# Local attention of the last two layers: value halves shifted by DMA, and the rotation of q and k one step earlier, around the softmax's reciprocal

## The reference, cut to what matters

```python
h = shift_token(x)
q, k, v = jnp.split(h @ wqkv, 3, axis=-1)          # 8 heads of 64
q = l2norm(q) * qs;  k = l2norm(k) * ksc
q, k = rotary_xpos(q, k)                            # q*cos*scale + rotate_half(q)*sin*scale
# windows of 64 queries; keys and values: the window and the one before it
sim = jnp.einsum('bhwid,bhwjd->bhwij', bq, bk)      # masked, bq carries QK_SCALE
attn = jax.nn.softmax(sim, axis=-1)
out = jnp.einsum('bhwij,bhwjd->bhwid', attn, bv)
x = x + out @ wo                                    # then the feed-forward
```

## Time and profile before

| | |
|---|---|
| median of 3 runs | 1512.03 us (1510.12 to 1512.65) |
| profiled execution | 1508.53 us, span 1506.5 us, mean granted TensorE clock 0.957 |
| PE busy | 1333.5 us, 89% of the span |
| DVE busy | 1013.3 us, 67% |
| ACT busy | 792.7 us, 53% |
| POOL busy | 361.6 us, 24% |

### The profile page before, as it was taken

The page is one execution under the profiler, slowest core; times in us unless marked ns, Lnnn a source line. Parts: engine busy times, 40 slices in busy tenths (PEclk is TensorE's granted clock), DMA queues, the critical chain, the costliest instruction groups (busy, mean ns, idle before and its releaser), DMA issues.

```text
span 1506.5 us, 23829 instructions
## 1 busy us (share of the span) xinstructions
PE 1333.5 (89%) x9009; PEld 790.8 (52%) x9009; DVE 1013.3 (67%) x2202; ACT 792.7 (53%) x1681; POOL 361.6 (24%) x288
## 2 busy tenths in 40 slices
PE   6999999999999999999589999987279988799886
PEld 4767677776777673333223333333146654366652
DVE  5767767687766856765577667740967775877755
ACT  4544435444444442434136666675169984499851
POOL 0000000011000003335410000000267771477732
PEclk9999999999999999999569999999589999999998
DMA  5000000000000000002023111100200000000000
GB/s 141 1 1 1 1 1 1 1 1 1 1 1 1 0 1 1 1 0 81 29 77 82 46 37 37 36 3 7 57 1 2 2 2 1 1 2 2 2 1 28
DMA packets 23725, 26.03 MB, mean 17 GB/s; under 512 B 5602, under 2 KB 20140, under 8 KB 22316
## 3 DMA queue, kind: packets, MB, share of 16 engines
q1 hardware_dynamic: 23612, 24.51, 5.5%
HBM read 20.11 MB, written 4.39 MB: 16 GB/s over the span
## 4 chain that ended last, share of the span: by engine, by line
PE 64%; ACT 14%; DVE 13%; issue 4%; POOL 2%; DMA 2%; SPq 0%; POOLq 0%; DVEq 0%; ACTq 0%
PE ps L679 13%; PE ps L699 8%; PE ps L714 7%; ACT probsT L2283 6%; PE ps L1051 4%; PE ps L1010 4%; PE ps L1031 3%; DVE negmax L1437 2%; PE ps L888 2%; PE ps L882 2%; PE ps L1182 2%; PE ps L650 2%; ACT v_st L2253 2%; PE ps L1173 2%; PE ps L872 2%
## 5 line engine op out<-in xcount | busy, mean ns | idle before, releaser
L2208 ACT ACTIVATE probsT<-ps 128x512 f32<-128x512 f32 (+1 forms) x304 | 163.6, 576 | 103.7 <-PE ps L1035 91.6
L1437 DVE TENSOR_REDUCE negmax<-ps 128x1 f32<-128x1024 f32 x128 | 150.7, 1219 | 72.5 <-PE ps L699 72.4
L2030 ACT ACTIVATE probs<-ps,negmax 128x1024 f32<-128x1024 f32 x128 | 142.5, 1114 | 80.5 <-DVE negmax L1437 76.5
L2036 ACT COPY probsT<-ps 128x512 f32<-128x512 f32 x128 | 74.8, 584 | 168.2 <-PE ps L714 168.1
L714 PEld LDWEIGHTS ps<-ident,probs 128*128 128x128 f32 x1024 | 114.5, 141 | 66.2 <-issue 44.0
L714 PE MATMUL ps<-ident,probs 128*128 128x128 f32 x1024 | 138.4, 277 | 6.6 <-DVE probsT L1450 3.4
L2360 POOL TENSOR_SCALAR rstd<-mv 128x4 f32<-128x4 f32 (+1 forms) x23 | 5.3, 233 | 578.5 <-DVE mv L1372 578.4
L1010 PE MATMUL ps<-arena 76*128 76x512 bf16 (+3 forms) x384 | 113.6, 355 | 26.4 <-DVE cmax L1705 20.6
L699 PE MATMUL ps<-k_st,q_st 64*128 64x512 f32 x512 | 128.7, 622 | 5.9 <-ACT probs L2030 5.9
L1705 DVE CUSTOM_DVE_ANT_0 k_st<-ps,rel 128x256 f32<-128x256 f32 (+7 forms) x128 | 96.8, 756 | 44.1 <-PE ps L1010 43.2
L1705 DVE CUSTOM_DVE_ANT_0 q_st<-ps,rel 128x256 f32<-128x256 f32 (+7 forms) x128 | 96.7, 756 | 41.9 <-PE ps L1010 41.0
(11 more groups left out here) (245 smaller groups left out, 2565.1 us busy)
## 6 DMA issues: line engine op xcount, KB each, us to landing
arena<-c_parts SPq DMA_DIRECT2D x32, 192.0 KB
arena<-c_parts SPq DMA_DIRECT2D x16, 128.0 KB
arena<-in_L_ffn_w_dram SPq DMA_DIRECT2D x3, 512.0 KB
c_parts<-probsT SPq DMA_DIRECT2D x2, 768.0 KB, 3.5
arena<-in_c_far_dram SPq DMA_DIRECT2D x16, 96.0 KB
c_parts<-work SPq DMA_DIRECT2D x2, 768.0 KB, 11.3
work<-in_L_ffn_wqkv_dram SPq DMA_DIRECT2D x1, 1536.0 KB
x_sb<-in_L_attn_x_dram SPq DMA_DIRECT2D x2, 512.0 KB, 5.9
```

Of the source, the lines that this page charges most:

```text
L1437: dve.tensor_reduce(negmax[:, u:u + 1], s2, AX_X, ALU.max, negate=True).then_inc(s_a_negmax, 1)
L2030: act.activation(probs[:, u % NPB, :], s2, ACT.Exp, bias=negmax[:, u:u + 1], accum_out=rowsum[:, u:u + 1]).then_inc(s_a_exp, 1)
L2208: act.activation(c_p[:, kt % 2, j0:j0 + heads, q0 - kt * P:q0 - kt * P + n], ps[:, 4 + c % 2, 0:heads * n].rearrange("p (h n) -> p h n", n ...
```

## The change

Three things are changed, in the last two layers alone. ScalarE no longer fills `d_vs`: SyncE does it with two DMAs of 64 rows x 512 for each tile, both from `d_va`, and ScalarE, the value product and the DMAs wait for each other by a new semaphore `s_d_vs`. The rotation on VectorE is moved from the start of step t (tile t+2) to its end (tile t+3), waits for the projection and no longer for the squares, and the reciprocal of tile t stands between its first product and its other two. The square on ScalarE is moved from the end of step t (tile t+3) to the place behind the value copy (tile t+2), and waits for the rotation. With them, PE's wait for the copies of the turned queries and keys stands behind the mask instead of ahead of it, GpSimd's sum of the queries is moved to the end of its step (tile t+3), and the pieces at the start of a layer follow.

```diff
@@ sync
+            for l in range(DEPTH):
+                for t in range(TILES):
+                    n, par = TILES * l + t, t % 2
+                    sp.wait_ge(s_d_v, n + 1)
+                    if exists(t, -2):
+                        sp.wait_ge(s_d_o, n - 1)
+                    if n:
+                        sp.wait_ge(s_d_vs, shifted(n))
+                    sp.dma_start(d_vs[0:WIN, par, :], d_va[0:WIN, par, :]).then_inc(s_d_vs, 16)
+                    if exists(t, -1):
+                        sp.dma_start(d_vs[WIN:P, par, :], d_va[WIN:P, 1 - par, :]).then_inc(s_d_vs, 16)
@@ tensor, step
-                        pe.wait_ge(s_d_qT, n + 1)
-                        pe.wait_ge(s_d_kT, n + 1)
...
+                        pe.wait_ge(s_d_qT, n + 1)
+                        pe.wait_ge(s_d_kT, n + 1)
                         for h in range(H2):
...
                         pe.wait_ge(s_d_pT, n)
+                        pe.wait_ge(s_d_vs, shifted(n))
@@ vector, rotate
-                    dve.wait_ge(s_d_sq, n + 1)
+                    dve.wait_ge(s_d_qkp, n + 1)
...
                     dve.tensor_tensor(mA, qk, heads(rot_c[:, t:t + 1, :, :]), ALU.mult)
+                    if between:
+                        between()
                     for d, e in ((0, 32), (32, 0)):
@@ vector, step
-                    if exists(t, 2):
-                        rotate(l, t + 2)
+                    def inverse():
+                        dve.wait_ge(s_d_e, n + 1)
+                        dve.reciprocal(d_rr[:, par, :], d_sum[:, par, :]).then_inc(s_d_rr, 1)
...
                         add_keys(l, t + 2)
-                        norms(l, t + 2)
                     if exists(t, -2):
...
+                    if exists(t, 2):
+                        norms(l, t + 2)
                     if piece:
                         piece()
-                    if exists(t, 0):
-                        dve.wait_ge(s_d_e, n + 1)
-                        dve.reciprocal(d_rr[:, par, :], d_sum[:, par, :]).then_inc(s_d_rr, 1)
+                    if exists(t, 3):
+                        rotate(l, t + 3, inverse)
+                    elif exists(t, 0):
+                        inverse()
@@ scalar, square and step
-                    act.wait_ge(s_d_qkp, n + 1)
+                    act.wait_ge(s_d_m, n + 1)
...
-                        if exists(t, -1):
-                            act.wait_ge(s_d_v, n)
-                            act.copy(d_vs[WIN:P, par, :], d_va[WIN:P, 1 - par, :])
                         act.wait_ge(s_d_vp, n + 1)
-                        act.copy(d_va[:, par, :], ps[:, 3, :])
-                        act.copy(d_vs[0:WIN, par, :], ps[0:WIN, 3, :]).then_inc(s_d_v, 1)
+                        if n >= 2:
+                            act.wait_ge(s_d_vs, shifted(n))
+                        if exists(t, -2):
+                            act.wait_ge(s_d_o, n - 1)
+                        act.copy(d_va[:, par, :], ps[:, 3, :]).then_inc(s_d_v, 1)
+                    if exists(t, 2):
+                        square(l, t + 2)
...
-                    if exists(t, 3):
-                        square(l, t + 3)
@@ gpsimd
+            def add_queries(l, t):
+                    n, par = TILES * l + t, t % 2
+                    kq = d_kq[par]
+                    pool.wait_ge(s_d_m, n + 1)
+                    if exists(t, -2):
+                        pool.wait_ge(s_d_qkt, n - 1)
+                    pool.tensor_tensor(kq[:, 0:INNER], d_mA[:, par, 0:INNER], d_mB[:, par, 0:INNER], ALU.add)\
+                        .then_inc(s_d_add, 1)
...
                     if exists(t, 2):
                         unit_norm(l, t + 2)
+                    if exists(t, 3):
+                        add_queries(l, t + 3)
```

More of the change, by code:

```diff
@@ L424, in build @@
         s_d_addk = sem("s_d_addk")
+        s_d_vs = sem("s_d_vs")
         s_d_s = sem("s_d_s")
@@ L455, in build, with exists, shifted @@
         block = ctx.enter_context(nc.Block())
+        def exists(t, shift):
+            return 0 <= t + shift < TILES
+        def shifted(n):
+            return 16 * (2 * n - (n + TILES - 1) // TILES)
         @block.sync
@@ L561, in build @@
         NU = 2 * QT
-        def exists(t, shift):
-            return 0 <= t + shift < TILES
         def ring(j):
@@ L1765, in tables, with rotate @@
                                                   sc[:, n:n + 1, e:e + 32].to_broadcast([P, QT, 32]), ALU.mult))
-            def rotate(l, t):
+            def rotate(l, t, between=None):
                     n, par = TILES * l + t, t % 2
@@ L1787, in add_keys @@
                     n, par = TILES * l + t, t % 2
+                    if exists(t, -2):
+                        dve.wait_ge(s_d_qkt, n - 1)
                     dve.wait_ge(s_d_m, n + 1)
@@ L1793, in norms @@
                     n, par = TILES * l + t, t % 2
+                    dve.wait_ge(s_d_sq, n + 1)
                     dve.tensor_reduce(ss[:, par, :], d_sq[:, par, :].rearrange("p (h d) -> p h d", d=HD2),
@@ L1889, in _ @@
             norms(0, 1)
+            rotate(0, 2)
             for l in range(DEPTH):
@@ L1938, in _ @@
                     add_keys(l + 1, 0)
-                    norms(l + 1, 0)
                 gated(l, 10)
                 if not last:
+                    norms(l + 1, 0)
                     next_shift(l, 1)
@@ L1958, in _ @@
                     next_shift(l, 2)
+                    rotate(l + 1, 2)
                     next_shift(l, 3)
@@ L2309, in _ @@
                 if l == 0:
-                    for t in range(3):
+                    for t in range(2):
                         square(l, t)
@@ L2330, in _ @@
                     if l + 1 < DEPTH:
-                        if j == 8:
+                        if j == 9:
                             square(l + 1, 0)
@@ L2335, in _ @@
                     act.activation(tpre[:, 1:2], eps_c[:, 0:1], ACT.Exp)
-                    square(l + 1, 2)
         @block.gpsimd
@@ L2478, in _ @@
             pool.wait_ge(s_d_init, 1)
-            def unit_norm(l, t):
+            def add_queries(l, t):
                     n, par = TILES * l + t, t % 2
@@ L2484, in unit_norm @@
                     pool.wait_ge(s_d_m, n + 1)
+                    if exists(t, -2):
+                        pool.wait_ge(s_d_qkt, n - 1)
                     pool.tensor_tensor(kq[:, 0:INNER], d_mA[:, par, 0:INNER], d_mB[:, par, 0:INNER], ALU.add)\
                         .then_inc(s_d_add, 1)
+            def unit_norm(l, t):
+                    n, par = TILES * l + t, t % 2
                     pool.wait_ge(s_d_cl, n + 1)
@@ L2489, in unit_norm @@
                     pool.wait_ge(s_d_addk, n + 1)
+                    pool.wait_ge(s_d_add, n + 1)
                     pool.wait_ge(s_d_rn, n + 1)
-                    v = kq[:, INNER:2 * INNER].rearrange("p (h d) -> p h d", d=HD2)
+                    v = d_kq[par][:, INNER:2 * INNER].rearrange("p (h d) -> p h d", d=HD2)
                     pool.tensor_tensor(v, v, d_rn[:, par, H2:2 * H2].unsqueeze(2).to_broadcast([P, H2, HD2]), ALU.mult)\
@@ L2496, in step, with begin @@
                     n, par = TILES * l + t, t % 2
-                    if exists(t, 0):
-                        v = d_p[:, par, :, :]
-                        pool.wait_ge(s_d_rr, n + 1)
-                        pool.tensor_tensor(v, v, d_rr[:, par, :].unsqueeze(2).to_broadcast([P, H2, P]), ALU.mult)\
-                            .then_inc(s_d_p, 1)
+                    v = d_p[:, par, :, :]
+                    pool.wait_ge(s_d_rr, n + 1)
+                    pool.tensor_tensor(v, v, d_rr[:, par, :].unsqueeze(2).to_broadcast([P, H2, P]), ALU.mult)\
+                        .then_inc(s_d_p, 1)
                     if exists(t, 2):
                         unit_norm(l, t + 2)
-            unit_norm(0, 0)
-            unit_norm(0, 1)
+                    if exists(t, 3):
+                        add_queries(l, t + 3)
+            def begin(l):
+                add_queries(l, 0)
+                unit_norm(l, 0)
+                add_queries(l, 1)
+                unit_norm(l, 1)
+                add_queries(l, 2)
+            begin(0)
             for l in range(DEPTH):
@@ L2515, in _ @@
                 if l + 1 < DEPTH:
-                    unit_norm(l + 1, 0)
-                    unit_norm(l + 1, 1)
+                    begin(l + 1)
             for c in range(NCH):
```

## The result

The median of four runs is 1492.20 us (1490.93 to 1493.52), against 1512.12 before: 19.9 us less, a ratio of 0.9871 with a 95% interval of 0.9854 to 0.9888. The forecast was 1485, its range 1480 to 1497. The change is 1.3% faster, clear of the scatter, by three quarters of what was forecast.

The account below looks back on a forecast made before the run. No engine is full; a loop of waits through ScalarE and TensorE sets the 9.04 us step. Gains 17.8 (24 steps) + 2.4 + 2.5 + 4.2 = 26.9 us off the median 1512.03 give 1485, range 1480 to 1497.

Parts of the forecast that it names:

- the steady steps: The 24 evenly spaced steps of both layers: each falls from 9.04 to 8.3 us, 17.8 us in all.
- the ends: Start of layer 0, passage into layer 1 and late steps of both layers: 2.4, 2.5 and 4.2 us gained.
- point 4: Steady step: TensorE's own work and the chain through ScalarE's two copies meet at the next scores; new length 8.3 us.
- Square and copies: Steady step: square (0.90 us) hidden in ScalarE's wait; two 64-row copies (0.63, at most 0.58) only make room for it.
- the near row: Profile row of a 256 KB DMA taking 2.3 us, taken for each new 128 KB DMA, which would be hidden.
- The rival in which they arrive late: Value copy waits for DMA landings, decisive above 8.4 us: 1515 to 1530, or about 1575; 5%.
- The late reciprocal: Steady step: reciprocal delayed, so probabilities come late; step 8.5 us and 1490, or 8.8 and 1497; 20%.
- The tails: Steps 14 and 15 of each layer: 2.1 us gained a layer, 4.2 in all.
- Point 11: Steps 14 and 15: mask off the path gives 0.5 us each, ScalarE's two copies 1.1 in step 15; 2.1 a layer.
- points 9 and 10: Start of layer 0 and passage into layer 1: squares and masks leave the path, 2.4 and 2.5 us gained.
- Point 9: Start of layer 0: square (0.90) and tile 1's mask (1.01) off the way, tile 0's mask (0.52) too; 2.4 us.
- The joint: Passage from layer 0 to 1: two rotations no longer wait for squares (1.9 us), plus 0.6 for three smaller items; 2.5 us.

Follow-up runs that it names:

- Mask alone: Kernel before, with only TensorE's wait for the copies of turned queries and keys moved behind the mask: 1498.75 us, ratio 0.9915.
- mask undone: Changed kernel with TensorE's wait for the copies of turned queries and keys moved back ahead of the mask: 1503.95 us, ratio 0.9948.
- DMAs alone: Kernel before, with only the two DMAs filling the shifted values in place of ScalarE's two 64-row copies: 1506.44 us, ratio 0.9970.
- e13: Not a run: a time mark, the start of tile 13's first exponential on ScalarE, in each layer.
- e14: Not a run: a time mark, the start of tile 14's first exponential on ScalarE, in each layer.
- three edits: Changed kernel with reciprocal ahead of the rotation, norm clamp on GpSimd, and the very first square ahead of its rotation: 1483.21 us, ratio 0.9812.
- e15: Not a run: a time mark, the start of tile 15's first exponential on ScalarE, in each layer.
- clamp on GpSimd: Changed kernel with the clamp of the norms on GpSimd, right ahead of the power, instead of on VectorE: 1489.57 us, ratio 0.9858.
- reciprocal last: Changed kernel with the reciprocal behind all three products of the rotation: 1500.18 us, ratio 0.9924.
- first square first: Changed kernel where, for the first tile of layer 0 only, the square waits for the projection and the rotation for the square: 1490.68 us.
- e0: Not a run: a time mark, the start of tile 0's first exponential on ScalarE, in each layer.
- e1: Not a run: a time mark, the start of tile 1's first exponential on ScalarE, in each layer.

## Why the prediction was right, and where it was not

The median lies in the range, and the steady steps carried it: of 17.8 us forecast for 24 steps 16.1 came, of 9.1 us forecast for the ends 0.9, and 1.0 more at a place that had no term. That so weak an account of the ends still ended in the range is owed to the width that the range had for the rivals.

- **The steady step, right.** 8.3 was forecast and 8.30 and 8.28 measured; 22 steps gave 16.5 us, 0.75 each. Both chains of point 4 are in the profile: the mask runs in the wait for ACT's copies, and PE is busy in 99% of the window. Mask alone and mask undone are 0.50 and 0.44 us a step, near its own 0.52.
- **Square and copies, right in kind.** The square is hidden (ACT waits 0.71 behind it). That the two copies "only make the room for the square" missed 0.13 us, as the DMAs alone show.
- **DMAs, right.** They land in 2.4 us, near the 2.3 of the near row and the 2.3 that I estimated from the Trainium skill (DMA: Bandwidth & Descriptors, Anatomy of one DMA), although that section gives its fit for DMAs issued by GpSimd and these are SyncE's. No engine waits for one. The rival in which they arrive late never came near its 8.4 us.
- **The late reciprocal.** It had 20%, and was there in one step of three. The clamp did wait for the query sum; the Trainium skill's rule (SBUF — State Buffer, Who interferes with whom), that an SBUF-to-SBUF operation of one input in a fast mode and a GpSimd operation keep each other off for a whole instruction, agrees with the trace: the clamp took 1.10 and ended with the query sum, the second shift copy took 1.41, 1.40 and 1.21 beside GpSimd's sums and scalings and 0.42 without. It did not hold beside GpSimd's power: the shift copy at 1282.12 took 0.42 inside a power that ran from 1281.87 for 3.01 us. The cost in the steady steps was 0.07 us, not the 0.2 of the forecast's step of 8.5.
- **The tails, wrong.** Point 11 forecast 2.1 us a layer and nothing was gained (+1.0, +0.3), and the 12th step, counted among the steady ones, lost 0.2 and 0.3 instead of gaining 0.7. Together that is 7.4 us of the 8.9 by which the sum, 26.9, missed the block's 18.0. Two things in it failed.

First, it took the feed-forward's pieces over from before unchanged: I had seen for the clamp that GpSimd can hold VectorE up, and not for the shift copies that follow it at the same place, nor for the scaling of the maxima in step 14. e13 to e14 was 9.5 before and 9.0 by point 11. With a long shift copy and a scaling of 0.17 it is 9.78 (three edits, clock 1.00), with both long 10.53 (layer 0 of the change).

Second, points 9 and 10 reckon with PE's half clock and point 11 does not. Windows from e14 to e15: layer 0 before; layers 0 and 1 of the change; layer 0 with the clamp on GpSimd (columns as for the steady step):

```profile
1234.39:1247.24 12.85, 7.41 (x114) 5.57 (x113) 7.83 (x30) 8.81 (x26) 5.89 (x7) 1.00 0.01 2
...
1229.19:1241.99 12.80, 8.53 (x110) 6.38 (x111) 8.00 (x30) 7.48 (x23) 4.42 (x5) 0.87 0.05 12
1421.47:1433.95 12.48, 8.64 (x114) 6.99 (x113) 7.94 (x30) 7.49 (x24) 4.40 (x5) 0.86 0.01 1
...
1226.30:1237.38 11.08, 7.22 (x114) 5.61 (x113) 7.95 (x30) 7.49 (x24) 4.41 (x5) 1.00 0.07 15
```

At a granted clock of 1.00 the order of the change has 11.07 to 11.09 us here, in all four places where that happened (both layers with the clamp on GpSimd, layer 1 with the reciprocal last and with the three edits). That is 1.8 less than the 12.85 before, so the 1.6 of point 11 for step 15 was right, and the half clock hid it. Step 14 of layer 1 lost to it too: clock 0.85 and 11.39 us. The kernel before lost 1.2 us in step 15 of layer 1 (14.02 at 0.88). By my estimate from these rows the clock is 3.4 of the 5.5 us that the two tails missed.

It may in part be the change's. Ahead of the second chunk in step 14 PE waits 1.1 to 1.4 us in the kernel before and with mask or DMAs alone, and came back at full speed in all six places; where the wait was 1.8 to 2.4 us it came back at half in 6 of 17. Why in these and not in the others stays open.

- **The head, half.** Point 9 forecast 2.4 and 1.2 was measured. It counted the square that goes and not the one that comes: tile 0's square was hidden behind VectorE's tables, and now stands between its rotation and the second projection, 1.1 us. Shown by the run with the first square first. The half clock from e0 to e1 cost the change another 1.0 us, and was made up for by more gain there than forecast (e0 to e1 is 7.51 at full clock; it was 10.31 before, at 0.83).
- **The joint, wrong in size.** 2.5 forecast, 1.0 measured. The rotations did come 2.1 us sooner (45.03 us after e15 before, 42.95 after, for that of tile 1), but of these only 1.2 reached the first maxima. VectorE, GpSimd and PE there, rows of three timelines:

```profile
1284.94 1.23 DVE L1799 TENSOR_TENSOR probs<-ps,arena 128x1024 f32<-128x1024 f32 x1 [0.96 <-PE ps L1148]
...
1294.15 1.18 DVE L1773 COPY arena<-xT 64x512 f32<-64x512 f32 x1
1295.35 1.64 DVE L1779 TENSOR_TENSOR arena<-arena 128x512 f32<-128x512 f32 x1
...
1293.86 1.18 POOL L2528 TENSOR_TENSOR k_st<-k_st,d_rn 128x512 f32<-128x512 f32 x1 [0.17 <-POOL d_rn L2523]
1295.00 1.45 POOL L2516 TENSOR_TENSOR q_st<-probs 128x512 f32<-128x512 f32 x1
...
1304.12 1.04 PE L1178 MATMUL ps<-rel,ident_b 128*128 128x512 bf16 x2 [5.36 <-ACT probsT L2315]
```

The copy (0.42 alone) and the table product (0.68 alone) each ran into a GpSimd instruction and lost 1.7 us between them; before the change one such collision was there already and cost 0.85 (L1764 at 1301.48 took 1.60, elsewhere 0.75), so 0.9 more was lost than before: the part of the 2.1 that is missing. And PE, idle for 5.36 us, did the mask of tile 1 at half speed, as the forecast had allowed for, but stayed there through the scores too: the granted clock from e0 to e1 of layer 1 is 0.64, 0.88 before.

- **The last stretch.** The 1.0 us after e15 of layer 1 was in no term. PE ran at half speed there before (value product and next projection 1.58 and 2.08 us) and not after (1.20 and 1.12). Ahead of it PE waited 1.80 us for ScalarE's 64-row copy before, and 0.56 for the value copy after. Over all kernels 2 of 6 such places with the wait of 1.80 fell to half speed, and none of the 22 with 0.56, so this may be a side effect of the DMAs; that is not shown. The 2.9 us ahead of the block are no effect of the change: that memset starts anywhere from 1072.5 to 1076.8 us in the profiled executions of the fourteen kernels.

## What to carry to other kernels

Work out the loop of the steady step first, chain by chain, and look for what stands in it by program order only: here two moved wait lines gave most of the gain. Then go through the ends with the same care, instruction by instruction, above all with those pieces that the change doesn't touch but that now run beside something else, and with a term for TensorE's clock wherever it has stood idle. And where a short instruction must precede a reciprocal or a maximum that others wait for, check what GpSimd reads at that moment.

## What the runs showed of the hardware that I had not expected

- Small VectorE instructions can last as long as the GpSimd instruction beside them: a 128x16 clamp 1.10 us instead of 0.17, an 8-column scaling of the maxima 0.96 instead of 0.17. Beside GpSimd's power of 128x16 (2.9 to 3.0 us) a shift copy kept its 0.42 us and the key sum of 128x512 its 0.68.
- ScalarE started the exponentials 0.48 us after the copy ahead of them in the kernels without its 64-row copies, and 0.61 after it in those with them, though the same two instructions stand there with the same waits. The cause stays open; it is worth 0.13 us a step here.
- After a wait of 3.0 us or more ahead of the normalised chunk of step 15 TensorE came back at half its speed, at once or within the next two groups, in 22 of 28 places (fourteen kernels, two layers), and at full speed in six; in one and the same kernel that is 12.71 against 11.09 us for the step (three edits, layers 0 and 1).
